# Selective scan: TensorE's sum of delta issued two replications later, ScalarE's reads of it in the next step

## What is computed

```python
dts = einsum('bkrl,kdr->bkdl', dts, dt_projs_weight)
delta = softplus(dts + dt_projs_bias[None, :, :, None])
def step(h, inp):
    u_t, d_t, B_t, C_t = inp
    h = exp(d_t[..., None] * A) * h + (d_t * u_t)[..., None] * B_t[:, :, None, :]
    y = einsum('bkdn,bkn->bkd', h, C_t)
    return (h, y)
```

## Time and profile before

| | before |
|---|---|
| median of 3 executions | 6398.05 us (6393.79 to 6409.08) |
| profiled execution, its own time | 6394.87 us |
| its span, first to last instruction | 6393.0 us |
| busy, whole span | PE 4941.9, DVE 4998.0, POOL 3864.0, ACT 2800.6 us |
| first scan starts, last two scans end | 3244.77 us, 6304.42 us |
| busy in 500 us of the scan (4500 to 5000) | DVE 443.35, POOL 387.86, PE 362.15, ACT 283.72 us |
[...]

### The profile page before, as it was taken

How to read it: one execution, slowest core, us unless ns; L and a number is a source line. 1 busy time by engine, 2 the same in 40 slices (tenths; PEclk the granted TensorE clock), 3 DMA queues, 4 the chain that set the end, 5 groups by cost and what they waited for, 6 DMA issues and landing times. The chain is left out here.

```text
span 6393.0 us, 70314 instructions
## 1 busy us (share of the span) xinstructions
PE 4941.9 (77%) x15250; PEld 2126.8 (33%) x15250; DVE 4998.0 (78%) x5048; ACT 2800.6 (44%) x4206; POOL 3864.0 (60%) x2394
## 2 busy tenths in 40 slices
PE   7999798976898889831967777777777777777777
PEld 1222264652665556520522222222222222222222
DVE  5777534343089999998978888898888898898886
ACT  5767444332000000000355555555555555555556
POOL 0000223224077789776867777777777777777773
PEclk9989899988998899865978888888888888888888
DMA  1000000017756665622156666666656666656653
GB/s 42 0 0 0 7 1 1 1 53 228 155 110 130 130 140 115 130 51 64 24 130 154 162 156 153 160 154 155 162 155 152 162 155 153 163 155 154 161 157 99
DMA packets 340808, 707.83 MB, mean 111 GB/s; under 512 B 46716, under 2 KB 63672, under 8 KB 326744
## 3 DMA queue, kind: packets, MB, share of 16 engines
q1 hardware_dynamic: 340568, 705.15, 44.7%
HBM read 572.97 MB, written 81.67 MB: 102 GB/s over the span
## 5 line engine op out<-in xcount | busy, mean ns | idle before, releaser
L1864 POOL TENSOR_TENSOR l_hc<-l_h,l_c_rep 128x512 f32<-128x512 f32 x1536 | 1935.8, 1271 | 668.1 <-DVE l_h L1917 656.4
L1917 DVE TENSOR_TENSOR_SCAN l_h<-l_p_da,l_h,l_bu 128x512 f32<-128x512 f32 x1344 | 1720.9, 1280 | 276.5 <-ACT l_p_da L1771 266.1
L1771 ACT ACTIVATE l_p_da<-l_p_da,l_a_neg 128x512 f32<-128x512 f32 x1536 | 993.8, 660 | 1318.1 <-PE l_p_da L1644 1306.4
L1146 POOL TENSOR_TENSOR l2b_prod<-l2b_v,l2b_attn 128x3136 f32<-128x3136 f32 x114 | 990.1, 8701 | 392.9 <-ACT l2b_attn L1138 369.8
L1644 PE MATMUL l_p_da<-l_stacked,l_pick 96*128 96x512 f32 x1536 | 868.2, 583 | 429.1 <-DVE l_h L1917 414.6
L1907 DVE TENSOR_TENSOR l_bu<-l_du_rep,l_p_b 128x512 f32<-128x512 f32 x1536 | 1021.9, 665 | 26.8 <-DMA l_du_rep<-du_scratch 21.1
L1644 PEld LDWEIGHTS l_p_da<-l_stacked,l_pick 96*128 96x128 f32 x1536 | 299.8, 202 | 1566.5 <-DVE l_h L1917 1357.1
L1180 DVE TENSOR_REDUCE l2b_osum<-l2b_prod 128x64 f32<-128x3136 f32 x192 | 645.9, 3414 | 2.7
L1652 PE MATMUL l_p_y<-l_hc,l_y_pick 128*32 128x512 f32 x3072 | 628.7, 695 | 8.0 <-POOL l_hc L1864 6.9
L1133 ACT ACTIVATE l2b_logits<-l2b_conv,l2b_this_b 98x512 f32<-98x512 f32 x96 | 66.1, 688 | 912.7 <-PE l2b_conv L1095 912.7
L615 POOL TENSOR_TENSOR l_w_pos_low<-l1a_w_sed,l_w_pos_high 96x1536 fp32r<-96x1536 f32 x1 | 4.1, 4120 | 712.7 <-DVE l_w_fc_high L595 712.7
(11 more groups left out here) (255 smaller groups left out, 8209.6 us busy)
## 6 DMA issues: line engine op xcount, KB each, us to landing
l_du_rep<-du_scratch SPq DMA_DIRECT2D x1536, 256.0 KB, 4.3
l2b_img_high<-qkv_scratch SPq DMA_DIRECT2D x192, 306.2 KB, 5.5
l2b_img_low<-qkv_scratch SPq DMA_DIRECT2D x192, 306.2 KB, 9.1
l_stacked<-l_parts SPq DMA_DIRECT2D x512, 96.0 KB, 3.1
qkv_scratch<-l2a_strip SPq DMA_DIRECT2D x32, 840.0 KB, 5.1
l2b_v<-qkv_scratch SPq DMA_DIRECT2D x48, 560.0 KB, 16.9
du_scratch<-l_du SPq DMA_DIRECT2D x128, 192.0 KB, 2.1
qkv_scratch<-l2a_v_strip SPq DMA_DIRECT2D x32, 210.0 KB, 4.0
```

Source lines behind the costliest of these rows:

```text
L1146: return eng.tensor_tensor(dst.rearrange("q x (dy dx) -> q x dy dx", dx=WIN), window, attn[:, :, r].rearrange("q x (dy dx) -> q x dy dx", ...
L1771: act.activation(p_da[i % DAS][:], p_da[i % DAS][:], ACT.Exp, scale=a_neg[:, k * G + GRP[i]:k * G + GRP[i] + 1]).then_inc(s_da, 1)
L1864: pool.tensor_tensor(hc[:, (G * par + i) % HCS, :], h[:, i, :], c_rep[:, par, :], ALU.mult).then_inc(s_hc, 1)
L1917: dve.tensor_tensor_scan(h[:, i, way], p_da[i % DAS][:, way], bu[:, i % BUS, way], state, ALU.mult, ALU.add).then_inc(s_h, 1)
```

## The change

Three lists change, and SyncE's order.

- PE: delta_sum(n+2) goes from behind i = 8 to behind i = 10, after y_triple(n, 1).
- ACT: delta_and_high(n+2) leaves step n (behind i = 10) and is issued in step n+1 behind i = 0. Ahead of the first step it is issued for m = 0 alone; that of m = 1 comes in step 0.
- POOL: rest(n+2) goes from behind i = 6 to behind i = 5, and delta_u(n+1) from in front of i = 2 to in front of i = 1.
- SyncE: replicate_du(n, 8 to 11) first, then restack(n+1), then store_du(n+1).

No operation is added or removed.

```diff
--- before.py
+++ after.py
@@ -1574,13 +1574,11 @@
             def step(n, par, more):
                 for i in range(RING, G):
                     replicate_du(n, par, i)
-                    if more and i == RING:
-                        store_du(n + 1, 1 - par)
-                    if more and i == RING + 1:
-                        sp_.wait_ge(s_rep, G * n)
-                        sp_.nop(nofuse=True)
-                        restack(n + 1, 1 - par)
                 if more:
+                    sp_.wait_ge(s_rep, G * n)
+                    sp_.nop(nofuse=True)
+                    restack(n + 1, 1 - par)
+                    store_du(n + 1, 1 - par)
                     for i in range(RING):
                         replicate_du(n + 1, 1 - par, i)
 
@@ -1688,10 +1686,10 @@
                         c_mm(n + 1, *n1, n2)
                     if i == 6:
                         y_triple(n, 0, par)
-                    if n2 and i == 8:
-                        delta_sum(n + 2, n + 2)
                     if i == 9:
                         y_triple(n, 1, par)
+                    if n2 and i == 10:
+                        delta_sum(n + 2, n + 2)
 
             def stack_count(b, k, c, par):
                 per = 16 * PARTS * 2
@@ -1804,8 +1802,8 @@
                         c_copy(n + 1, 1 - par)
                     if before and i == 7:
                         take_y(n - 1, *before, 1 - par)
-                    if n2 and i == 10:
-                        delta_and_high(n + 2, par)
+                    if n1 and i == 0:
+                        delta_and_high(n + 1, 1 - par)
                     if k == 0 and i == 8:
                         if not isinstance(c, int):
                             turn_x(b, c + 2)
@@ -1822,8 +1820,8 @@
                 one_plus(m)
                 kept(m)
                 log_1e(m)
-                delta_and_high(m, m)
                 if m == 0:
+                    delta_and_high(0, 0)
                     c_copy(0, 0)
             all_steps(step)(act)
             take_y(B * STEPS - 1, B - 1, K - 1, CHUNKS - 1, 1)
@@ -1870,10 +1868,10 @@
                 for i in range(G):
                     if n1 and i == 0:
                         low(n + 1, 1 - par)
-                    if n1 and i == 2:
+                    if n1 and i == 1:
                         delta_u(n + 1, *n1)
                     times_c(n, i, par)
-                    if n2 and i == 6:
+                    if n2 and i == 5:
                         rest(n + 2)
 
             rest(0)
```

## The result

| | before | changed |
|---|---|---|
| median of 4 executions | 6396.31 us | 6123.57 us (6120.17 to 6131.78) |
| profiled execution, its own time | 6394.87 us | 6131.78 us |
| first scan to the end of the last | 3059.65 us | 2788.87 us |
| idle time in front of scans | 324.8 us | 64.6 us |

The ratio is 0.9572, with a 95% interval of 0.9555 to 0.9588. The forecast was 6060 us with a range of 6042 to 6120: the direction and the mechanism are right, the gain is 273 us where 336 were expected, and the time lies 4 us above the range.

What follows compares the result with a forecast made beforehand. VectorE's scans set the pace, with holes from TensorE's wait for rest_e. Holes of 347.9 us less 126 x 0.1 for the clock, plus 1.3 at the start, make 336 us less: 6060 us, range 6042 to 6120.

Steps and rivals of the forecast that it cites:

- The cause and the ceiling: PE's wait of 3.08 us for rest_e stalls DVE's scans; holes total 347.9 us, stage without them 2711.8 us.
- The margin of rest_e: On POOL, rest_e would be ready 2.4 us before PE's sum behind replication 10 needs it, ending the wait.
- delta_u, SyncE's order: POOL's earlier delta_u fits its load; SyncE's reordered DMAs leave du tiles 5.8 us to spare; cost nothing.
- The start: ACT no longer reads the second delta before the first decay, so scan 0 starts some 1.3 us earlier.
- dt_mm was to start no later than before: On PE behind replication 1, dt_mm would not be delayed by ACT's moved reads; cost nothing.
- The cover of 2.79 us: How late any replication on PE may start without holding up its scan on DVE.
- the clock's cost: PE at half clock from y_triple through replication 11 delays scans by 0 to 1.35 us a step; 0.1 taken.
- today's slow stretch begins in the idleness that goes: PE's clock falls shortly after it goes idle for rest_e, a wait of 3.08 us that the change removes.
- a slow stretch seldom covers triple, sum and replication 11 together: The worst needs PE slow from 10.6 to 18.3 us; 1.53 us of cover left absorbs most partial overlaps.
- the bound of 1.35: With PE slow from y_triple on, replication 11 starts at 18.32 us, 1.35 past the cover, in each step.
- the latest time that the cover allowed: Replication 11 may start as late as z + 16.97 us, z being the start of replication 3 on PE.
- Rival 1: Part of the stall stays, from PE's slow clock or POOL falling behind; up to 6230 us, chance 0.11 above 6080.

Runs made afterwards that it cites:

- e1: Changed kernel with one extra float32 matmul of relu_x on TensorE behind each of replications 7 and 8, result overwritten: 6053.6 us.
- e8: Kernel before with only the sum of delta taken apart (relu_x behind replication 7, log_e behind 8, rest_e behind 10): 6057.8 us.
- e5: Changed kernel with POOL's part undone (rest behind product 6, delta_u in front of product 2): 6117.8 us.
- e6: Changed kernel with SyncE's order undone (store of du and restack between the replication DMAs again): 6122.7 us.
- e4: Changed kernel with ACT's part undone, reading the sum behind decay 10 of the same step: 6181.8 us.
- e3: Changed kernel with TensorE's part undone, the whole sum of delta behind replication 8 again: 6213.3 us.
- e2: Changed kernel with the sum of delta taken apart (relu_x behind replication 7, log_e behind 8, rest_e behind 10): 6060.3 us.

## Why the prediction was wrong

**Right.** *The cause and the ceiling.* The wait for rest_e, with the sum in front of the next replications, made the stall, and the stage without holes was put at 2711.8 us; e1 has 2718.3, e8 2719.9. *The margin of rest_e*, 2.4 us: no wait is left, nor with POOL's part undone. *delta_u, SyncE's order*: nothing, and e5 and e6 confirm it. *The start* was to give 1.3 us: scan 0 waits 2.61 us where it had waited 3.47. But e4, which undoes that edit, waits 2.96 and e1, which keeps it, 2.94, so this gain is not shown.

**Wrong in a detail that cost nothing.** dt_mm was to start no later than before. It waits about 1.0 us in 100 of the steps in the window. Even in e1's step, with the clock at 1.00, it waits 0.79 us: behind the end of parts come some 0.7 us until PE starts (4521.55 to 4522.23), which I had left out, and replication 0 is late where the sum was slow. The cover of 2.79 us took it: in the whole of e1 the idle times in front of scans 1 and 2 add up to 1.0 us. That ACT's move itself is worth 58 us I had not priced.

**The step that failed** is a term of the sum: the clock's cost, which the prediction bounded by 0 and 1.35 us a step and put at 0.1. It measured 66 / 126 = 0.53 by the holes in front of scan 11, and 0.56 by what e1's fillers took away, (2788.9 - 2718.3) / 126. The 77 us above 2711.8 aren't all the clock's: e1 keeps 6.5 of them. 0.53 in place of 0.1 is 54 us, most of the 64 by which the forecast missed; the rest stays open, and the start of the scan alone varies by more than that.

The text gave two reasons for a value near 0. One was that today's slow stretch begins in the idleness that goes. That idleness was not what the fall needed. The mean of 0.59 in the earlier trace rows puts the fall at 4503.18, 0.21 us after PE went idle at 4502.97, and in 15 of the 126 steps of the kernel before the fall comes ahead of the wait, by up to 0.27 us. What stands ahead of the fall is the thin stretch, in which PE was busy for 0.68 of the 1.95 us from 4500.00 to 4501.95, still at 1.00; that stretch stayed. (It also grew, from replications 7 and 8 to 7 to 9, but it need not have: e3 has it at its old length and a mean clock of 0.835.) The other reason was that a slow stretch seldom covers triple, sum and replication 11 together, and that the cover absorbs the partial cases. In the changed kernel the mean clock over the first part of the sum was under 0.75 in 105 of the 126 steps, over the third in 80, and 79 had a hole. The fact had been seen and written down (the last row has 4 us at 0.50 with PE busy for 3.02) and was then given a tenth of its weight.

**Right in part by luck.** The largest hole is 1.31 us by the brackets, near the bound of 1.35, but two terms of that bound were wrong and nearly cancelled. From the start of the y triple to that of replication 11 it had 1.93 + 0.71 + 1.91 + 2.42 = 6.97 us, a sum of durations that overlap in the trace; the holed step has 4779.81 - 4774.30 = 5.51. From there to the end of decay 11 it took the 1.20 us of full speed; at the lower clock it is 2.11. Replication 11 started 0.1 us ahead of the latest time that the cover allowed (z was 4762.94, and z + 16.97 is 4779.91), and scan 11 was still 0.94 us late: the cover itself shrinks at the lower clock. Rival 1, which named this mechanism and the range 6075 to 6230, got 0.11; it is what happened, at some 40% of its full size (66 of 170 us).

**Idleness and the clock in the changed kernel.** From 3300 to 5950 us the granted clock fell 129 times. In the 7 us ahead of 127 of these falls no idleness between PE's recorded matmuls was over 1.3 us; ahead of the other two the longest were 2.0 and 2.8 us. And between 4730 and 4738 PE was busy for 7.99 of 8 us, at a mean clock of 0.50. So with the wait of 3.08 us gone the clock still fell, and a busy PE stood at the lower clock.

## What to carry to other kernels

When a long wait of TensorE is taken away, look at what the clock does in the work around it, and price that work at the lower clock (here 1.91 us where the same part took 1.02) unless the rows show otherwise. A block of several matmuls whose operands become ready at different times need not stay together: issue each part where its operand is ready and the engine has little to do, and only the late part keeps the late place. That gave the whole gain with one edit (e8), where moving the block whole needed a second engine's list changed and left a fifth of it behind. It moved the slow stretch of the clock and did not remove it (e2).

## What the runs showed of the hardware

In e1 adding work made the kernel faster: two more float32 matmuls a step took the granted clock of the scan from a mean of 0.832 to 0.962 and the time down by 70 us. The same work in another order (e2) left the mean where it was, 0.826, and moved the slow stretches to another part of the step. The matmul of the float32r part took 0.71 us at a clock of 0.50 behind a PE idle for 3.08 us, and 1.42 us, also at 0.50, right behind others in the changed kernel, so here the duration from the idle moment was no bound for the busy one; from its start to that of the next it was 1.21 us there (4778.89 - 4777.68). And the engine in the brackets was not the cause: half of the changed kernel's idle time in front of scans (32.9 of 64.6 us) carried POOL's name and went away in e1 without a change on POOL.
